# Edge sort: where and when the passed rows are marked

## The chip, the cores and the metric

The kernel runs on one core of a Trainium2 chip. The metric is the device time of one execution in microseconds; lower is better.

## The reference

```python
# x: 6250 nodes x 256; src, dst: 106250 edges
edge_index = stack([src, dst])
def gnn(X, (row, col)):
    denom = max(segment_sum(1, row), 1)
    neigh_mean = segment_sum(X[col], row) / denom
    H = relu(X @ W_root + neigh_mean @ W_neigh + b)
    diffs = abs(H[row] - H[col]) ** 2
    return tanh(segment_sum(diffs, row) / denom)
x = x + gnn(layernorm(x), edge_index)
x = x + mixture_of_experts(layernorm(x))   # router, 6 experts of 3 layers, the best 2 combined
```

Edges arrive sorted by `dst` and are summed by `src`, so the kernel first sorts them itself.

## The kernel before

The nodes lie in 49 blocks of 128. The kernel has four stages, one after the other: the edge sort (to about 297 us), a first pass over 842 tiles of 128 edges that sums neighbours, a second pass over the same tiles that sums squared differences, and the experts. In both passes GpSimd gathers the rows of a tile by an indirect DMA, VectorE makes a one-hot matrix, TensorE multiplies, VectorE adds the product to the block's sums.

The change is in the edge sort. The edges stand as 128 lanes by 832 columns. After ranks are found (VectorE, GpSimd and ScalarE, to about 105 us), the edges are put in order chunk by chunk. There are `C` = 8 chunks with two halves each, `CC` = 16 lists. `dve_edges` (line 858) runs 64 steps `k` of `BT` = 13 columns; four steps (`t` = 0 to 3) make a list. In a step VectorE makes three one-hot operands: `is_col` (line 993), `hot_lane` (line 997) and `hot_col` (line 1001; ScalarE makes 8 of its 13 upper columns, line 812). TensorE multiplies them into a list in PSUM (line 728). At `t` = 2 of the next list VectorE and ScalarE move the finished list to SBUF (`dve_list`, line 1123; `act_low`, line 856). At `k` = 3 VectorE also makes the variances of the nodes (lines 1194 to 1181).

Each list has 512 rows of 16 edges, 4 groups (`GG`) of 128. A row's place in DRAM depends on which blocks begin before it. For each of the first 8 chunks VectorE marks, for 98 half blocks and 512 rows, three times whether the row number has passed a start (`dve_passed`, line 1117, one instruction of 98 x 1536 in step `t` = 0). TensorE multiplies the marks with the jumps of the row numbers (`pe_rows`, line 776, at `t` = 1), and VectorE sums that to places (`dve_rows`, lines 1131 and 1134, at `t` = 3). All chunks use one tile `passed`.

GpSimd (`pool_edges`, line 582) makes 14 of the 49 bucket masks (line 649), the counting rows `count_h` (line 653), and then scatters: for each of 16 lists, it waits for places and list, and issues 4 indirect DMAs of 128 rows each to DRAM, which add (line 663). 64 scatters in all. Lists alternate between two DRAM tables. After the last, SyncE loads the two tables back (`sp_list`), TensorE turns them, VectorE makes indices, and GpSimd's first gather starts (line 1276).

SyncE meanwhile writes the normalised rows for the gathers (line 1141), four blocks at a time, and behind each of the first ten writes it clears a part of the sums' tile `big` (`sp_clear`, lines 561 and 563). The parts lie behind `sorting_end`, where the working tiles of the sort end. VectorE clears the rest after the sort (line 1211).

The order on every engine is that of the program; engines are tied by semaphores alone.

Of the kernel before, what the change touches and what calls it, by code (L numbers as in the profile page):

```python
# [38 lines left out]
def gnn_moe_kernel(nc, x, x_cols, x_cols_last, src, dst, w_root, w_neigh, b_gnn, rw1, rb1, rw2, rb2,  # L39
# [66 lines left out]
    with ExitStack() as ctx:  # L106
# [121 lines left out]
        passed = carve_sort(3 * GG * P // 2).bitcast(F16).rearrange("p (j r) -> p j r", j=3)  # L228
# [12 lines left out]
        sorting_end = at  # L241
        assert codes_at + 2 * NT <= sorting_end
# [22 lines left out]
        def turned_at(k):  # L265

            bank, place = divmod(k + per - 1, per)
            return ps[bank][:, place * P if bank else 0:][:, 0:min(P, NT - list_blocks[k] * P)]
        by_block = acc.rearrange("p (b w) -> p b w", w=W2)
# [154 lines left out]
        s_passed = sem("passed_rows_marked")  # L424
        s_jumped = sem("row_jumps_summed")
# [130 lines left out]
        assert clear_parts < len(z_sets)  # L556

        def sp_clear(e, i):
            if i == 0:
                e.wait_ge(s_pick, NB)  # L560
                e.dma_start(acc[:, NB * W2 - clear_over:NB * W2], local[:, 0:clear_over]).then_inc(s_cleared, 16)
            a, z = i * CLEAR_BY, min((i + 1) * CLEAR_BY, clear_times)
            e.dma_start(acc[:, sorting_end + a * NTR:sorting_end + z * NTR].rearrange("p (n w) -> p n w", w=NTR),
                        local.unsqueeze(1).to_broadcast([P, z - a, NTR])).then_inc(s_cleared, 16)
# [17 lines left out]
        def pool_edges(e):  # L582
# [71 lines left out]
            e.iota(far, [[CODE, MIX]], base=0, channel_multiplier=CODE * ((N - MIX) // P), **ALL_ONE).then_inc(s_region, 1)  # L654
            for c in range(CC):
# [114 lines left out]
        def pe_rows(e, c):  # L770
            e.wait_ge(s_passed, c + 1)
            if c:
                e.wait_ge(s_dest, c)
            for g in range(GG):
                for j in range(3):
                    m = e.matmul(ps[6][:, 4 * g:4 * g + 4], passed[0:NB2, j, g * P:(g + 1) * P],
# [81 lines left out]
        def dve_edges(e):  # L858
# [125 lines left out]
            e.tensor_scalar(at_rank, iota[0:NB, 0:NB], block_t[0:NB, 4:5], None, ALU.is_equal).then_inc(s_jump, 1)  # L984
            e.tensor_copy(code_f, high[:, :, 0]).then_inc(s_code, 1)
            e.wait_ge(s_wide, 1)
            for k in range(TW // BT):
# [15 lines left out]
                if t == 0 and c < C:  # L1003
                    dve_passed(e, c)
# [107 lines left out]
        def dve_passed(e, c):  # L1112
            if c == 0:
# [3 lines left out]
            e.tensor_tensor(passed[0:NB2, :, :].rearrange("p j (r q) -> p j r q", q=2),  # L1117
                            count_h[0:NB2, :].rearrange("p (r q) -> p r q", q=2).unsqueeze(1).to_broadcast(every),
                            starts_two[:, :, c, :].unsqueeze(2).to_broadcast(every), ALU.is_ge).then_inc(s_passed, 1)
# [1296 lines left out]
```

## Time and profile before

| | |
|---|---|
| median of 3 runs | 2837.13 us (2836.13 to 2838.58) |
| profiled execution | 2836.03 us, its span 2834.2 us |
| busy in the span | TensorE 81%, GpSimd 72%, VectorE 70%, ScalarE 31% |
| masks and ranks end, steps begin | 111.7 us |
| first scatter, last scatter begin | 134.14 us, 289.89 us |
| first gather of the first pass | 297.14 us |

The shares are means over stages with different limits; a stage has to be read from its own rows. An instruction's idle time before it names what released it; "issue" is time for which the profile shows no wait. Overlapping starts (an instruction that begins 0.08 us before the one ahead of it ends) are usual on VectorE, so costs on its path are taken from start to start.

### The profile page before, as it was taken

The numbers are of one execution on the slowest core, as the hardware profiler recorded it, in microseconds if no ns is written. First come the engines' busy times: TensorE is split into PE (matmuls) and PEld (weight loads), VectorE is DVE, ScalarE is ACT, GpSimd is POOL, SyncE is SP. The second block draws the span as 40 slices with busy tenths as digits, with TensorE's granted clock in tenths as the row PEclk, the third lists the DMA queues.
The fourth block names the chain that finished last, engine by engine and source line by source line (L and its number), as shares of the span: only waits on it lengthen the run. The fifth ranks groups of instructions, "written<-read, shape, count | busy, mean of one in ns | idle before, by whom it ended". The sixth has DMA issues, their size and how long they took to land.

```text
span 2834.2 us, 33557 instructions
## 1 busy us (share of the span) xinstructions
PE 2298.4 (81%) x8655; PEld 1296.3 (46%) x8655; DVE 1993.5 (70%) x5304; ACT 872.4 (31%) x2404; POOL 2030.8 (72%) x2021
## 2 busy tenths in 40 slices
PE   6676577777777777777789898888998888899996
PEld 4564444454434444444233333333333333389996
DVE  8997555556655555555578888888888888755456
ACT  7897000001100000000233333333333333355553
POOL 2488777777777777777677777777777766667772
PEclk8598789987677776766899999999999999999998
DMA  4254333334433333333543434344434333332266
GB/s 128 92 143 81 95 106 106 105 106 120 127 105 113 112 113 105 113 112 113 173 119 112 126 118 126 112 124 117 126 112 123 117 93 112 104 102 94 90 190 207
DMA packets 173026, 332.36 MB, mean 117 GB/s; under 512 B 45296, under 2 KB 108636, under 8 KB 172578
## 3 DMA queue, kind: packets, MB, share of 16 engines
q0 software_dynamic: 100224, 249.16, 30.6%
q1 hardware_dynamic: 70306, 78.94, 8.5%
q10 hardware_dynamic: 2304, 2.10, 0.2%
q8 instruction: 71, 1.16, 0.2%
q14 instruction: 121, 0.99, 0.1%
HBM read 279.94 MB, written 40.96 MB: 113 GB/s over the span
## 4 chain that ended last, share of the span: by engine, by line
DVE 28%; PE 24%; POOL 17%; issue 13%; DMA 10%; DVEq 6%; ACT 1%; SPq 0%; POOLq 0%; ACTq 0%
DVE big L1369 19%; PE ps L1320 15%; POOL arena L1276 11%; DMA arena<-xn_table,graph 7%; DVEq L1333 6%; PE ps L2294 5%; POOL edge_list L663 4%; DVE graph L1363 4%; PE ps L2276 3%; DMA arena<-h_table,graph 2%; POOL arena L1803 1%; PE ps L1379 1%; POOL y_by_token L1809 1%; PE ps L2244 1%; DVE big L872 1%
## 5 line engine op out<-in xcount | busy, mean ns | idle before, releaser
L1320 PE MATMUL ps<-arena,graph 128*128 128x258 f32 (+3 forms) x3956 | 1672.7, 593 | 405.9 <-DVE graph L1363 383.8
L1320 PEld LDWEIGHTS ps<-arena,graph 128*128 128x128 f32 (+1 forms) x3956 | 749.9, 223 | 1286.5 <-DVE graph L1363 1025.6
L1369 DVE TENSOR_TENSOR big<-ps,big 128x258 f32 (+1 forms) x1978 | 1100.2, 556 | 112.9 <-PE ps L1320 78.1
L1276 POOL DMA_INDIRECT arena<-h_table,graph x842 | 819.2, 973 | 287.9 <-issue 155.9
L1276 POOL DMA_INDIRECT arena<-xn_table,graph x842 | 799.0, 949 | 261.9 <-issue 191.9
L1363 DVE TENSOR_SCALAR graph<-iota,graph 128x128 f32<-128x128 f32 x1684 | 506.1, 301 | 509.9 <-DMA arena<-xn_table,graph 311.1
L1300 ACT ACTIVATE arena<-arena 128x256 f32<-128x256 f32 x842 | 348.5, 416 | 694.6 <-DMA arena<-h_table,graph 636.0
L1290 ACT ACTIVATE late<-late 128x256 f32<-128x256 f32 x49 | 20.3, 415 | 995.9 <-DVE late L1445 995.9
L1809 POOL DMA_INDIRECT y_by_token<-big,node x106 | 121.0, 1141 | 71.9 <-DVE big L1864 55.1
L663 POOL DMA_INDIRECT edge_list<-big x64 | 138.1, 2158 | 42.9 <-issue 42.3
L1803 POOL DMA_INDIRECT arena<-xn_table,node x106 | 111.8, 1055 | 39.4 <-issue 31.4
L812 ACT ACTIVATE big<-arena,big 128x64 f16<-128x64 f16 x512 | 129.7, 360 | 13.7 <-DVE arena L993 13.5
L1864 DVE TENSOR_TENSOR big<-ps,node 128x256 f32<-128x256 f32 x106 | 45.0, 424 | 118.9 <-PE ps L2276 118.3
L2276 PE MATMUL ps<-node,big 128*128 (+1 forms) x448 | 116.1, 382 | 5.9 <-DVE big L1864 3.5
L2294 PE MATMUL ps<-arena 128*128 128x128 f32 x848 | 114.6, 279 | 0.7 <-ACT big L2183 0.4
L2294 PE MATMUL ps<-big,arena 128*128 128x128 f32 x848 | 112.7, 276 | 0.0
L2294 PEld LDWEIGHTS ps<-arena 128*128 128x128 f32 x848 | 105.3, 195 | 1.9 <-issue 1.7
L2294 PEld LDWEIGHTS ps<-big,arena 128*128 128x128 f32 x848 | 104.0, 193 | 0.0
L728 PE MATMUL ps<-big,arena 128*128 128x128 f16 x832 | 67.7, 239 | 40.8 <-ACT big L812 27.6
L728 PEld LDWEIGHTS ps<-big,arena 128*128 128x128 f16 x832 | 57.2, 108 | 62.1 <-issue 49.8
L1840 DVE COPY arena<-node 128x1028 f32 x106 | 74.4, 703 | 15.4 <-ACT big L2191 6.5
L2276 PEld LDWEIGHTS ps<-node,big 128*128 128x128 f32 x448 | 76.5, 191 | 13.4 <-issue 6.4
(330 smaller groups left out, 1579.3 us busy)
## 6 DMA issues: line engine op xcount, KB each, us to landing
arena<-xn_table,graph POOLq DMA_INDIRECT x842, 2.8
arena<-h_table,graph POOLq DMA_INDIRECT x842, 2.8
big<-y_by_token SPq DMA_DIRECT2D x48, 256.0 KB, 4.4
big<-graph SPq DMA_DIRECT2D x10, 848.0 KB
h_table<-late SPq DMA_DIRECT2D x49, 128.0 KB, 2.1
late<-h_table SPq DMA_DIRECT2D x49, 128.0 KB, 3.0
xn_table<-late SPq DMA_DIRECT2D x12, 512.0 KB
big<-in_x SPq DMA_DIRECT2D x48, 128.0 KB, 2.6
```

What stands on the lines that cost most here:

```text
L663: e.indirect_dma_start(out=edge_list[c % 2], out_offset=bass.IndirectOffsetOnAxis(ap=dest[:, c, g:g + 1], axis=0), in_=lists[:, c, g * R8: ...
L812: e.activation(hot_col[:, r, u, 0, :], is_col[:, r, u, :], ACT.Copy, scale=code_f[:, t0 + u:t0 + u + 1]).then_inc(s_hcola, 1)
L1276: e.indirect_dma_start(out=row, out_offset=None, in_=table, in_offset=bass.IndirectOffsetOnAxis(ap=idx[:, t:t + 1], axis=0)).then_inc(s_ro ...
L1300: e.activation(rows2[:, sq, :], rows2[:, slot, :], ACT.Square).then_inc(s_sq, 1)
L1320: e.matmul(out_, hot[part, g % HOTS, :], moving, start=True, stop=True).then_inc(s_sum[i], 1)
L1333: _, places = nc.values_load_multi_w_load_instructions(offs[0:1, a:z], engines=[mybir.EngineType.DVE], min_val=0, max_val=(NB - 1) * W2, s ...
L1363: e.tensor_scalar(hot[:, g % HOTS, :], iota[:, :], local[:, t:t + 1], None, ALU.is_equal).then_inc(s_hot[i], 1)
L1369: e.tensor_tensor(block, ps[a % n_banks][:, 0:width], block, ALU.add)._wait_ge(s_sum[i], a + 1).then_inc(s_add[i], 1)
L1803: e.indirect_dma_start(out=xg[:, k % XR, :], out_offset=None, in_=xn_table, in_offset=bass.IndirectOffsetOnAxis(ap=tok[:, k:k + 1], axis=0 ...
L1809: e.indirect_dma_start(out=y_table, out_offset=bass.IndirectOffsetOnAxis(ap=y_row[:, k:k + 1], axis=0), in_=y_out[:, k % YB, :], in_offset ...
L2276: m = e.matmul(ps[3][:, 0:D], h2[:, n % 2, j * P:(j + 1) * P], last_of[j], start=(j == 0), stop=(j == KH - 1))
L2294: t = e.matmul(bank[:, m * P:(m + 1) * P], weights_of(k, at_, P), moving[:, j * P:(j + 1) * P], start=(j == 0), stop=(j == KD - 1))
```

## The change

- Each of the 8 chunks gets marks of its own, `passed(c)`, in `big` behind `sorting_end`, 768 words per chunk. A copy of the starts in float32, `starts_f`, lies behind them.
- VectorE copies the starts (one instruction of 98 x 24 ahead of the first step) and marks chunks 0, 1 and 2 in steps `k` = 0, 1, 2, with the same instruction as before (`mark_passed`).
- GpSimd marks chunks 3 to 7, after `count_h` and ahead of its first scatter: three `tensor_scalar` of 98 x 512 per chunk, 15 in all.
- `pe_rows` waits for one semaphore or the other, by chunk.
- The parts cleared by SyncE come in another order: parts 4 to 9, then 0 to 3, and before part 0 (issued behind the seventh write) SyncE waits until the row products of all 8 chunks are made.

```diff
--- before.py
+++ after.py
@@ -225,7 +225,6 @@
         dest_f = carve_sort(2 * GG).rearrange("p (h g) -> p h g", h=2)
         dest = carve_sort(CC * GG).bitcast(U32).rearrange("p (c g) -> p c g", c=CC)
         count_h = carve_sort(GG * P // 2).bitcast(F16)
-        passed = carve_sort(3 * GG * P // 2).bitcast(F16).rearrange("p (j r) -> p j r", j=3)
         ends_t = carve_sort(NB2)
         seen = carve_sort((STEP_COLS + UNITS) * NB)[0:STEP_ROWS, :]
         seen_whole = seen[:, 0:STEP_COLS * NB].rearrange("p (r b) -> p r b", b=NB)
@@ -239,6 +238,9 @@
         code_f = carve_sort(TW)
         hot_col = carve_sort(BT * 2 * HI).bitcast(F16).rearrange("p (r t a m) -> p r t a m", r=2, t=BT, a=2)
         sorting_end = at
+        PASSED_EARLY = 3
+        passed_words = 3 * GG * P // 2
+        assert sorting_end + C * passed_words <= NB * W2
         assert codes_at + 2 * NT <= sorting_end
         assert PR == ZR and 2 * KD * D + ZR * D <= 6 * KD * D and Z_AT + NB < TW // BT
         XAT = -(-taken // D)
@@ -266,6 +268,13 @@
 
             bank, place = divmod(k + per - 1, per)
             return ps[bank][:, place * P if bank else 0:][:, 0:min(P, NT - list_blocks[k] * P)]
+        starts_f = big[0:NB2, sorting_end + C * passed_words:sorting_end + C * passed_words + 3 * C].rearrange(
+            "p (j c) -> p j c", j=3)
+
+        def passed(c):
+            at_ = sorting_end + c * passed_words
+            return big[0:NB2, at_:at_ + passed_words].bitcast(F16).rearrange("p (j r) -> p j r", j=3)
+
         by_block = acc.rearrange("p (b w) -> p b w", w=W2)
 
 
@@ -422,6 +431,7 @@
         s_kept = sem("sums_of_units_kept")
         s_jump = sem("row_jumps_and_ends_made")
         s_passed = sem("passed_rows_marked")
+        s_passed_p = sem("passed_rows_marked_by_pool")
         s_jumped = sem("row_jumps_summed")
         s_dest = sem("list_rows_made")
         s_scat = [sem(f"rows_scattered_{i}") for i in range(2)]
@@ -554,11 +564,16 @@
         clear_times, clear_over = divmod(NB * W2 - sorting_end, NTR)
         clear_parts = -(-clear_times // CLEAR_BY)
         assert clear_parts < len(z_sets)
+        PASSED_PARTS = -(-(C * passed_words + 3 * C) // (CLEAR_BY * NTR))
+        assert PASSED_PARTS < clear_parts
 
         def sp_clear(e, i):
             if i == 0:
                 e.wait_ge(s_pick, NB)
                 e.dma_start(acc[:, NB * W2 - clear_over:NB * W2], local[:, 0:clear_over]).then_inc(s_cleared, 16)
+            i = (i + PASSED_PARTS) % clear_parts
+            if i == 0:
+                e.wait_ge(s_jumped, C)
             a, z = i * CLEAR_BY, min((i + 1) * CLEAR_BY, clear_times)
             e.dma_start(acc[:, sorting_end + a * NTR:sorting_end + z * NTR].rearrange("p (n w) -> p n w", w=NTR),
                         local.unsqueeze(1).to_broadcast([P, z - a, NTR])).then_inc(s_cleared, 16)
@@ -652,6 +667,12 @@
             e.wait_ge(s_pick, NB)
             e.iota(count_h, [[1, GG * P]], base=0, channel_multiplier=0, **ALL_ONE).then_inc(s_region, 1)
             e.iota(far, [[CODE, MIX]], base=0, channel_multiplier=CODE * ((N - MIX) // P), **ALL_ONE).then_inc(s_region, 1)
+            e.wait_ge(s_jump, 6)
+            e.wait_ge(s_region, 11)
+            for c in range(PASSED_EARLY, C):
+                for j in range(3):
+                    e.tensor_scalar(passed(c)[:, j, :], count_h[0:NB2, :], starts_f[:, j, c:c + 1], None,
+                                    ALU.is_ge).then_inc(s_passed_p, 1)
             for c in range(CC):
                 e.wait_ge(s_dest, min(c, C - 1) + 1)
                 e.wait_ge(s_list, c + 1)
@@ -768,12 +789,15 @@
             m.then_inc(s_zP, 1)
 
         def pe_rows(e, c):
-            e.wait_ge(s_passed, c + 1)
+            if c < PASSED_EARLY:
+                e.wait_ge(s_passed, c + 1)
+            else:
+                e.wait_ge(s_passed_p, 3 * (c - PASSED_EARLY + 1))
             if c:
                 e.wait_ge(s_dest, c)
             for g in range(GG):
                 for j in range(3):
-                    m = e.matmul(ps[6][:, 4 * g:4 * g + 4], passed[0:NB2, j, g * P:(g + 1) * P],
+                    m = e.matmul(ps[6][:, 4 * g:4 * g + 4], passed(c)[:, j, g * P:(g + 1) * P],
                                  jumps[:, j, c, :, :].rearrange("p h d -> p (h d)"), start=(j == 0), stop=(j == 2))
             m.then_inc(s_jumped, 1)
 
@@ -982,6 +1006,7 @@
 
             e.tensor_scalar(ends_t[0:NB2, :], ident[0:NB2, 0:NB2], end_of, None, ALU.mult).then_inc(s_jump, 1)
             e.tensor_scalar(at_rank, iota[0:NB, 0:NB], block_t[0:NB, 4:5], None, ALU.is_equal).then_inc(s_jump, 1)
+            e.tensor_copy(starts_f, starts_two[:, :, :, 0]).then_inc(s_jump, 1)
             e.tensor_copy(code_f, high[:, :, 0]).then_inc(s_code, 1)
             e.wait_ge(s_wide, 1)
             for k in range(TW // BT):
@@ -1000,8 +1025,8 @@
                 for i, part, u in ((0, high, BY_ACT), (1, low, 0)):
                     e.tensor_tensor(paired(hot_col[:, r, u:BT, i, :]), paired(is_col[:, r, u:BT, :]),
                                     across(part, t0 + u, BT - u, HI), ALU.mult).then_inc(s_hcold, 1)
-                if t == 0 and c < C:
-                    dve_passed(e, c)
+                if k < PASSED_EARLY:
+                    mark_passed(e, k, s_passed)
                 if t == 2 and c:
                     dve_list(e, c - 1)
                 if t == 3 and c < C:
@@ -1109,14 +1134,14 @@
                 e.tensor_tensor(jumps[:, :, :, :, d], a.unsqueeze(3).to_broadcast([NB2, 3, C, 2]), halves,
                                 ALU.mult).then_inc(s_jump, 1)
 
-        def dve_passed(e, c):
+        def mark_passed(e, c, made):
             if c == 0:
                 e.wait_ge(s_region, 11)
                 e.wait_ge(s_jump, 3)
             every = [NB2, 3, GG * P // 2, 2]
-            e.tensor_tensor(passed[0:NB2, :, :].rearrange("p j (r q) -> p j r q", q=2),
+            e.tensor_tensor(passed(c).rearrange("p j (r q) -> p j r q", q=2),
                             count_h[0:NB2, :].rearrange("p (r q) -> p r q", q=2).unsqueeze(1).to_broadcast(every),
-                            starts_two[:, :, c, :].unsqueeze(2).to_broadcast(every), ALU.is_ge).then_inc(s_passed, 1)
+                            starts_two[:, :, c, :].unsqueeze(2).to_broadcast(every), ALU.is_ge).then_inc(made, 1)
 
         def dve_list(e, c):
             e.wait_ge(s_lowp, c + 1)
```

## Rows read from the trace of the kernel before

**Rows 1.** Stretch in us, its length; busy us (count) of PE, PEld, DVE, ACT, POOL; clock, DMA.

```profile
255.00:297.00 42.00, 14.21 (x108) 12.25 (x108) 13.54 (x29) 12.58 (x52) 30.95 (x19) 0.54 0.29 25
```

**Rows 2.** Chain of waits between 110 and 300 us, shares by line.

```profile
by line: POOL edge_list L663 60.7%; issue 25.0%; DMA edge_list<-big 6.2%; DVE big L1001 1.7%; DMA big<-edge_list 1.3%; DVE arena L993 1.1%; DVE arena L979 1.0%; DVE big L1029 0.6%; DVE big L1023 0.6%; DVE big L1117 0.5%; PE ps L742 0.4%; DV
```

**Rows 3.** GpSimd in order: start us, us, what, [idle before]; last, its 64 scatters (min/median/max ns).

```profile
134.14 3.02 POOL L663 DMA_INDIRECT edge_list<-big  x1 [23.74 <-issue]
...
139.65 4.90 POOL L663 DMA_INDIRECT edge_list<-big  x1 [0.30 <-issue]
...
149.11 5.42 POOL L663 DMA_INDIRECT edge_list<-big  x1 [0.30 <-issue]
...
189.02 5.42 POOL L663 DMA_INDIRECT edge_list<-big  x1 [0.30 <-issue]
...
194.75 2.00 POOL L663 DMA_INDIRECT edge_list<-big  x1 [0.31 <-issue]
...
254.80 1.55 POOL L663 DMA_INDIRECT edge_list<-big  x1 [0.30 <-issue]
...
289.89 1.55 POOL L663 DMA_INDIRECT edge_list<-big  x1 [0.30 <-issue]
...
297.14 1.02 POOL L1276 DMA_INDIRECT arena<-xn_table,graph  x1 [5.71 <-DVE graph L1231]
...
L663 POOL DMA_INDIRECT edge_list<-big x64: 1546/1871/5417, 134.1 to 289.9; - x64
```

**Rows 4.** Gathers of the first pass: duration min/median/max ns, first and last start us.

```profile
L1276 POOL DMA_INDIRECT arena<-xn_table,graph x842: 942/946/1179, 297.1 to 1351.3; - x169
```

**Rows 5.** VectorE in order of time, same columns as rows 3.

```profile
113.88 0.95 DVE L1117 TENSOR_TENSOR big<-big,small 98x1536 f16<-98x1536 f16 x1
...
114.75 0.58 DVE L993 TENSOR_TENSOR arena<-graph,arena 128x832 f16<-128x832 f16 x1
...
121.55 1.75 DVE L1194 BATCH_NORM_AGGREGATE mv<-stats 128x2 f32<-128x6 f32 x25
...
125.67 0.58 DVE L993 TENSOR_TENSOR arena<-graph,arena 128x832 f16<-128x832 f16 x1
...
133.06 0.22 DVE L1123 SCALAR_TENSOR_TENSOR big<-ps,big 128x64 f32<-128x64 f32 x1
...
147.80 0.95 DVE L1117 TENSOR_TENSOR big<-big,small 98x1536 f16<-98x1536 f16 x1
...
153.02 0.22 DVE L1123 SCALAR_TENSOR_TENSOR big<-ps,big 128x64 f32<-128x64 f32 x1
...
195.25 0.16 DVE L1131 SCALAR_TENSOR_TENSOR big<-ps,rownum 128x8 f32<-128x8 f32 x1
...
265.39 0.21 DVE L1123 SCALAR_TENSOR_TENSOR big<-ps,big 128x64 f32<-128x64 f32 x1
```

**Rows 6.** Masks on GpSimd, columns as in rows 4.

```profile
L649 POOL TENSOR_SCALAR arena<-node x10: 2286/2287/2325, 59.5 to 91.6; 128x832 f16<-128x832 f16 x10
```

**Rows 7.** ScalarE in order of time: its last instruction of a chunk.

```profile
209.56 0.22 ACT L856 ACTIVATE big<-ps 128x64 f32<-128x64 f32 x1
...
218.71 0.24 ACT L856 ACTIVATE big<-ps 128x64 f32<-128x64 f32 x1
```

**Rows 8.** SyncE in order of time: the seventh write of normalised rows.

```profile
203.26 0.37 SPq L1141 DMA_DIRECT2D xn_table<-late  x1
```

**Rows 9.** VectorE's column compare of all 64 steps, columns as in rows 4.

```profile
L993 DVE TENSOR_TENSOR arena<-graph,arena x64: 577/584/623, 111.7 to 265.5; 128x832 f16<-128x832 f16 x64
```

**Rows 10.** All engines in order of time, first 8 us.

```profile
1.19 1.27 DVE L862 CAST graph<-iota 128x128 f16<-128x128 f32 x1 [0.21 <-POOL iota L583]
...
6.42 0.18 POOL L619 MEMSET node<- 128x98 f32 x1
...
7.13 0.69 DVE L864 TENSOR_SCALAR node<-arena 128x832 int32<-128x832 int32 x1 [4.67 <-DMA arena<-in_dst]
...
7.41 0.54 POOL L629 MEMSET node<- 128x98 f32 x1
```

## The prediction

> **What bounds the kernel now.** I read the trace in four looks: the busy shares by stretch, the chain of waits over the sorting stage, GpSimd's instructions in order of time, and VectorE's and ScalarE's beside them.
>
> From 255 to 297 us GpSimd is busy for 31 of the 42 us and VectorE for only 13.5: the sort's own work is over, the scatters are behind [rows 1]. The chain runs mostly over the scatter line of GpSimd, 60.7% of its length between 110 and 300 us; the 0.3 us hand-overs between scatters appear there as "issue" [rows 2]. The first gather of the next stage follows the last scatter by a fixed tail: 289.89 + 1.55 = 291.44 us to 297.14 us, 5.7 us [rows 3]. That stage is GpSimd's too: 842 gathers from 297.1 to 1351.3 us, 1.25 us each with no room to catch up [rows 4]. So each microsecond by which the last scatter ends earlier or later should reach the end of the kernel whole.
>
> Inside the scatters there are two paces. From 134.14 to 194.75 us GpSimd issues 18, or 3.37 us each. From 194.75 to 254.80 it issues 27, or 2.22 us each, and the last eleven, with VectorE idle, come every 1.85 us. The slow part is made by six long ones: 4.90 us for the one at 139.65 and 5.42 us for the five others, of which 149.11 and 189.02 stand as first and last [rows 3]. Each starts 1.3 to 1.9 us after one of VectorE's eight marks of passed rows (line 1117, the mark at 147.80 for the scatter at 149.11), and ends 1.3 us after the next list instruction of VectorE (153.02 + 0.22 against 154.53) [rows 3, 5]. Behind the eighth and last mark comes one such scatter, that at 189.02, and then none. Between marks and long scatters the count is six for six. The other two marks lie ahead of the first scatter.
>
> **The change part by part.** *Marks that leave the scatters.* Six of eight marks now stand between scatters. In the changed kernel three are made in VectorE's steps 0 to 2, all ahead of the first scatter, and five by GpSimd, also ahead of it. A mark costs VectorE 0.87 us (113.88 to 114.75) [rows 5]; five fewer give 4.35 us. Ahead of the first list stand three instead of two, so that list comes 0.87 us later.
>
> *The copy of starts.* One cast of 98 x 24 on VectorE. The nearest row is an instruction of 128 x 8 with 0.16 us (195.25) [rows 5], about 0.1 us from start to start. The bounds are 0.05 and 0.25.
>
> *Fifteen marks on GpSimd.* The trace has no such instruction of 98 x 512 f16; the nearest is its compare of 128 x 832 f16, 2.287 us [rows 6]. In proportion to the columns that is 1.41 us; a small fixed part makes it more, and I take 1.47. The 832-column row itself, 2.29, is the upper end; a third of it, 0.76, is a lower end. Fifteen make 22.1 us (11.4 to 34.3). They start once the starts are copied, at about 111.5, and would end at 133.6. GpSimd has just this gap: it idles 23.74 us ahead of the scatter at 134.14 [rows 3]. So alone they cost nothing; if they took 2.29 us each, the scatters would begin 11 us late. TensorE's products for a chunk wait for these marks from step 13 on, after 145 us, so they are in time.
>
> *What the freed scatters do.* The list of chunk 0 moves from 133.06 to 134.03, and the first scatter, 1.08 us behind it as now [rows 3, 5], to 135.1. From there GpSimd needs 53 x 2.22 + 11 x 1.85 + 1.2 (its first is longer, 3.02 us) = 139.2 us, and would end at 274.3. But it can't be ahead of the lists. These come every 9.98 us now (133.06 to 153.02 is two), and without the mark VectorE needs 9.11; ScalarE needs 9.16 per chunk (209.56 to 218.71) [rows 5, 7] and becomes the slower by a hair, which takes back some 0.3 us of the 4.35. The list of chunk 14 moves from 265.39 to 265.39 - 4.35 + 0.1 + 0.3 = 261.4. Chunk 14's scatters then start at 262.5 and take 4 x 2.1 = 8.4, chunk 15's 4 x 1.85 = 7.4: end at 278.3. This is the later of the two, so it holds: 291.4 - 278.3 = 13.1 us less. The wait on VectorE's lists is what is late next. The lower and upper ends of this part are 17.1 (GpSimd's own pace) and, if GpSimd's marks run at 2.29 us, 291.4 - 285.4 = 6.0 (first scatter at 146.2, plus 139.2).
>
> *The order of the clears.* The same bytes are cleared by the same eleven DMAs; parts 4 to 9 come first, and the seventh, issued behind the write at 203.26, now waits until all eight row products are made. VectorE uses the eighth at 195.25 [rows 5, 8], so the wait is over 8 us before. Queued behind it on SyncE are the normalised rows' writes, which the first gather needs; were the wait late, they would be late by as much, with 80 us in hand. Zero.
>
> *Rows of their own.* A chunk's marks no longer overwrite those that TensorE reads; no wait was seen for that, so nothing is gained.
>
> *The sum.* The profiled execution took 2836.03 us (span 2834.2 and 1.8 around it). 2836.0 - 13.1 = 2822.9; the median of the runs, 2837.1, is 1.1 above the profiled one, so 2824.0.
>
> **What speaks against it: a shared way into the memory.** The scatters' lengths show that GpSimd waits for VectorE when it reads. The least of the 64 is 1.546 us and the last ones, alone, are as short; the median, beside VectorE's steps, is 1.871, and the long ones last until VectorE runs something else [rows 3]. In the other direction the trace shows little: VectorE's compare of 832 columns is 577 ns at the least and 623 at the most over all 64, with 45 scatters beside it [rows 9]; but a scatter reads only 128 offsets. At the start of the kernel both directions stand once. A GpSimd memset of 98 columns takes 0.54 us beside VectorE's shift of 832 columns, and 0.18 otherwise. A VectorE cast of 128 columns takes 1.27 us beside GpSimd's first memsets, where that shift of 832 takes 0.69 [rows 10]. A mark on GpSimd reads its 512 columns throughout, so it could shut VectorE out for its whole 1.47 us.
>
> The Trainium skill says so outright (SBUF — State Buffer, "Who interferes with whom"): a VectorE instruction with two SBUF inputs contends with a GpSimd instruction that reads SBUF, and whoever holds the shared pair keeps it for the whole instruction. The trace agrees for GpSimd's reads (1.546 against 1.871 us); for VectorE being held for a whole GpSimd compare no row here shows it, and by the rule the time would be that of the first rival below.
>
> **The rivals.**
> 1. *The two engines take turns (slower).* Every instruction of VectorE's steps has two inputs in SBUF. If each GpSimd mark holds one up for its length, VectorE loses 22.1 us before its first list, or 18.0 if marks lie beside the variances (121.55 to 125.67 [rows 5]), which mostly read one input. All lists move with it: the end of the scatters is 278.3 + 18.0 to 22.1 = 296.3 to 300.4, that is 4.9 to 9.0 us later than now. It decides from 13.1 us of hold-up, that is from 0.9 us per mark. For it: the rows above. Against it: VectorE's times beside 45 scatters. With 7.5 us: 2844.6.
> 2. *GpSimd starves.* It gets in once per step of 2.17 us. If VectorE loses nothing, 15 marks last 15 x 2.17 = 32.6 us, the first scatter starts at 144.4 and the last ends at 283.6, 7.8 us less than now: 2829. This is still my side of the line. If it is both starved and holds VectorE up (2.17 + 1.47 = 3.64 us per mark from step 4 on, if 8 are left then: 133.4 + 29.1), the first scatter starts near 162.5 and the last ends near 301.7: 2847.
> 3. *The marks are not what makes the scatters long.* Then three scatters pass per chunk for the first six chunks as now, at 9.11 instead of 9.98 us each: 5.2 less, 1.0 later start, so 4.2: 2833. Against it: the six-for-six count. It is also the case in which the change doesn't do what it says.
>
> **How the numbers follow.** Forecast, with the milder half of rival 2: 0.53, its own range 2820 to 2830. Rival 1: 0.29. The harsh half of rival 2: 0.06. Rival 3: 0.12. A measurement of this kernel can tell 0.2%, 5.7 us, from no change. Faster by more than that: the forecast's 0.53 and 0.02 of rival 3, 0.55. Within: the rest of rival 3 and a quarter of rival 1, 0.17. Slower: 0.28. The range 2819 to 2847 takes in both signs and leaves out the harsh end and gains above 18.
>
> **What would show it.** Right: no scatter above 2.5 us but the first; 15 GpSimd compares of about 1.5 us from 111.5 on, ended by 134; VectorE's 832-column compares still near 584 ns between 112 and 134; list of chunk 0 at 134; last scatter ended near 278; the gathers 13 us earlier with the same pace. Wrong by rival 1: instructions of VectorE between 112 and 145 that last up to 2 us, first list after 150. By rival 2: compares of GpSimd longer than 2 us. By rival 3: scatters of 5 us although no mark stands near them.

## The result, and the profile after

The changed kernel takes 2843.29 us (median of 11 runs, 2840.54 to 2846.14), the kernel before 2837.16 us in its runs beside it (11 runs, 2835.97 to 2844.02). The ratio is 1.0020 with a 95% interval of 1.0012 to 1.0028: slower, by 6.1 us where 13.1 us less were forecast. The profiled execution took 2841.83 us, its span 2840.1 us.

The busy shares by stretch answer to [rows 1]; the columns are the stretch and its length, then the busy time of TensorE, its weight loads, VectorE, ScalarE and GpSimd with the instructions in brackets, the granted clock, and the DMA share and rate.

```profile
110.00:134.00 24.00, 9.25 (x84) 7.85 (x85) 23.59 (x71) 12.20 (x49) 22.98 (x9) 0.50 0.66 268
255.00:297.00 42.00, 13.09 (x118) 11.37 (x118) 14.34 (x29) 14.29 (x60) 33.23 (x20) 0.60 0.25 15
```

GpSimd was to finish its fifteen marks in the first of these stretches. It has nine instructions there, seven of them marks, and is busy from the first mark on. At the end of the sort the picture is as before: VectorE is idle for two thirds of the stretch, and scatters are still being issued.

GpSimd in order of time answers to [rows 3] (start and duration in us, engine, line, operation, operands, count; in brackets its idle time before it and what ended that):

```profile
109.47 0.56 POOL L668 IOTA big<- 128x512 f16 x1
111.19 43.18 POOL L674 TENSOR_SCALAR big<-big 98x512 f16<-98x512 f16 x15 [1.02 <-DVE big L1009]
154.55 2.02 POOL L684 DMA_INDIRECT edge_list<-big  x1 [0.18 <-issue]
...
292.47 1.55 POOL L684 DMA_INDIRECT edge_list<-big  x1 [0.30 <-issue]
300.03 1.02 POOL L1301 DMA_INDIRECT arena<-xn_table,graph  x1 [6.01 <-DVE graph L1256]
```

The marks last 43.18 us instead of 22.1. The first scatter starts at 154.55, where 135.1 was forecast and 134.14 stood before; the last ends at 294.02 instead of 291.44, and the first gather starts at 300.03 instead of 297.14 [rows 3].

By line, with the least, the median and the longest duration in ns and the first and last start, the fifteen marks and the 64 scatters are:

```profile
L674 POOL TENSOR_SCALAR big<-big x15: 1559/2107/13136, 111.2 to 152.3; 98x512 f16<-98x512 f16 x15
L684 POOL DMA_INDIRECT edge_list<-big x64: 1546/1958/2227, 154.6 to 292.5; - x64
```

The long scatters of 5.42 us are gone, as forecast. What took their place is a first mark of 13.14 us and fourteen others of 2.1 us mostly; 1.56 us is the least. Cut down to its start, the first mark reads

```profile
111.19 13.14 POOL L674 TENSOR_SCALAR big<-big 98x512 f16<-98x512 f16 x1 [1.02 <-DVE big L1009]
```

and it ends at 124.33. VectorE beside it answers to [rows 5]:

```profile
110.92 0.16 DVE L1009 CAST big<-small 98x24 f32<-98x24 f16 x1
113.68 0.94 DVE L1142 TENSOR_TENSOR big<-big,small 98x1536 f16<-98x1536 f16 x1
...
119.76 0.94 DVE L1142 TENSOR_TENSOR big<-big,small 98x1536 f16<-98x1536 f16 x1
...
122.81 0.15 DVE L1156 SCALAR_TENSOR_TENSOR big<-ps,rownum 128x8 f32<-128x8 f32 x1
122.99 0.16 DVE L1159 TENSOR_TENSOR big<-big,ps 128x8 uint32<-128x8 f32 x1
...
125.38 0.53 DVE L1194 TENSOR_SCALAR nsc<-nsc 128x49 int32<-128x49 int32 x1
...
129.78 1.24 DVE L1026 TENSOR_TENSOR big<-arena 128x320 f16<-128x320 f16 x2
...
136.14 0.21 DVE L1148 SCALAR_TENSOR_TENSOR big<-ps,big 128x64 f32<-128x64 f32 x1
...
159.27 0.81 DVE L1026 TENSOR_TENSOR big<-arena 128x320 f16<-128x320 f16 x2
```

Two things are to be seen. First, from 111.19 to 122.96 VectorE's instructions follow each other with overlapping starts and the mark does not move. Between the row sum at 122.81 and the next at 122.99 there are 0.03 us in which VectorE runs nothing, and the mark ends 1.37 us after that. Counted from the start of the row sum at 122.81 it is 1.52 us. The long scatters of the kernel before end 1.50 to 1.51 us after the start of a list instruction (153.02 for the one at 149.11), and there the next instruction starts at 153.15, before the list instruction's 0.22 us are over [rows 3, 5]. So a gap of VectorE is not needed: what the list instruction and the row sum have in common is that they read PSUM and only one tile in SBUF. Second, once the marks do get in, VectorE is held up, but lightly: the pair of `hot_col` products takes 1.23 us beside a mark and 0.81 without one, and an instruction of the variances 0.53 instead of the usual 0.19. It is 0.34 to 0.43 us each time, and not the whole mark. The first mark of GpSimd starts 2.49 us ahead of VectorE's first (113.68), so it is already waiting when that one comes.

The chain of waits between 110 and 300 us, summed by line, answers to [rows 2]:

```profile
by line: POOL edge_list L684 53.5%; issue 19.1%; POOL big L674 12.1%; DMA edge_list<-big 4.0%; DVE big L1026 2.4%; DVE arena L1018 1.6%; DMA big<-edge_list 1.6%; DVE big L1142 1.4%; DVE arena L1003 1.0%; DVE mv L1219 0.9%; DVE nsc L1198 0.5
```

The scatter line fell from 60.7%, and the marks on GpSimd came in with 12.1%: between them they leave VectorE only single per cents.

### The profile page after: what moved, and what is told of

Its sections match the earlier page's. It is cut to its first block, busy times and chain, and to the rows that moved or that the text cites. A ratio compares the mean times of both kernels' runs of the same rounds, so it can differ in the third digit from the quotient of the medians.

```text
span 2840.1 us, 33570 instructions
## 1 busy us (share of the span) xinstructions
PE 2303.5 (81%) x8655; PEld 1299.7 (46%) x8655; DVE 1995.7 (70%) x5300; ACT 871.9 (31%) x2404; POOL 2056.0 (72%) x2036
## 4 chain that ended last, share of the span: by engine, by line
PE 29%; DVE 26%; POOL 16%; issue 12%; DMA 10%; DVEq 5%; ACT 1%; SPq 1%; ACTq 0%; POOLq 0%
PE ps L1345 18%; DVE big L1394 16%; POOL arena L1301 11%; DMA arena<-xn_table,graph 7%; PE ps L2319 6%; DVEq L1358 5%; POOL edge_list L684 4%; DVE graph L1388 3%; PE ps L2301 3%; DMA arena<-h_table,graph 2%; DMA big<-y_by_token 1%; POOL big L674 1%; PE ps L1404 1%; PE ps L2269 1%; PE ps L2344 1%
## 5 line engine op out<-in xcount | busy, mean ns | idle before, releaser
L1345 PE MATMUL ps<-arena,graph 128*128 128x258 f32 (+3 forms) x3956 | 1678.8, 591 | 401.0 <-DVE graph L1388 379.1
L836 ACT ACTIVATE big<-arena,big 128x64 f16<-128x64 f16 x512 | 129.7, 362 | 15.9 <-DVE arena L1018 15.7
L684 POOL DMA_INDIRECT edge_list<-big x64 | 120.3, 1879 | 19.4 <-issue 19.1
L749 PE MATMUL ps<-big,arena 128*128 128x128 f16 x832 | 66.2, 236 | 44.7 <-ACT big L836 15.7
```

The lines of the kernel that those rows point to most:

```text
L684: e.indirect_dma_start(out=edge_list[c % 2], out_offset=bass.IndirectOffsetOnAxis(ap=dest[:, c, g:g + 1], axis=0), in_=lists[:, c, g * R8: ...
L749: m = e.matmul(ps[4 + c % 2][:, 0:2 * HI], hot_lane[:, r, u, :], hot_col[:, r, u, :, :].rearrange("p a m -> p (a m)"), start=(t == 0 and u ...
L836: e.activation(hot_col[:, r, u, 0, :], is_col[:, r, u, :], ACT.Copy, scale=code_f[:, t0 + u:t0 + u + 1]).then_inc(s_hcola, 1)
L1345: e.matmul(out_, hot[part, g % HOTS, :], moving, start=True, stop=True).then_inc(s_sum[i], 1)
```

## The experiments

The theory after the result: GpSimd's reads of SBUF find a place only at certain instructions of VectorE. Three questions follow. Is it GpSimd's marks that cost the time (e1)? What in VectorE's mark shuts GpSimd out: its place (e2), its form with two inputs (e3), the lack of an instruction behind it that would break the run (e4)? Or is it that VectorE, whose mark waits for nothing, gets ahead of its own instruction stream, so that a next instruction always stands ready (x1 and what follows)?

The x and y kernels ran on two other chips, on which the kernel before takes 3160 us; so each ratio is against the kernel before on the same chip. There is no trace of the kernel before from those chips, and times inside the sort are compared across chips. That the sort keeps its times there is seen at x1, which has before's marks in before's places and starts its first scatter at 133.74 (134.14 before).

### e1: all eight chunks marked by VectorE ahead of the scatters

```diff
-        PASSED_EARLY = 3
+        PASSED_EARLY = 8
```

> The changed kernel with all eight chunks marked by VectorE, one in each of steps 0 to 7, and none by GpSimd. Theory A (GpSimd's marks wait for VectorE; a VectorE mark closes the way to GpSimd until VectorE's next instruction that is not a two-input one of the step): no starved marks, the first list 0.87 x 5 us after that of before (137.4), first scatter at 138.5, one long scatter at most (marks of steps 6 and 7), last scatter ended at 278 to 282 against 291.4 before and 294.0 changed: about 2837 - 11 = 2826 us. Theory B (the marks on VectorE are not what makes scatters long; any step does it while the first eight chunks run): the six long scatters stay, time 2837 to 2842 us.

Measured: 2829.5 us, ratio 0.9971 (0.9961 to 0.9982). GpSimd in order of time, and VectorE around the first scatter:

```profile
138.94 3.76 POOL L684 DMA_INDIRECT edge_list<-big  x1 [28.30 <-DVE big L1148]
...
280.46 1.55 POOL L684 DMA_INDIRECT edge_list<-big  x1 [0.30 <-issue]
287.95 1.02 POOL L1301 DMA_INDIRECT arena<-xn_table,graph  x1 [5.94 <-DVE graph L1256]
```

```profile
136.86 0.96 DVE L1142 TENSOR_TENSOR big<-big,small 98x1536 f16<-98x1536 f16 x1
137.73 0.23 DVE L1148 SCALAR_TENSOR_TENSOR big<-ps,big 128x64 f32<-128x64 f32 x1
...
140.04 0.96 DVE L1142 TENSOR_TENSOR big<-big,small 98x1536 f16<-98x1536 f16 x1
140.90 0.17 DVE L1156 SCALAR_TENSOR_TENSOR big<-ps,rownum 128x8 f32<-128x8 f32 x1
```

The half of the change that takes marks from between the scatters is worth 7.1 us of the kernel (2829.5 against 2836.6) and 9.2 at the first gather. So GpSimd's fifteen marks cost that gain and 6.1 us more. And two marks here stand beside the start of the scatters without making a 5 us one (the first scatter lasts 3.76 us): the list instruction or the row sums come directly behind them. The time of 2829.5 us lies above the 2826 expected, and the last scatter's end, 282.01, at the edge of 278 to 282.

### e2: the three VectorE marks ahead of the first step

```diff
+            for c in range(PASSED_EARLY):
+                mark_passed(e, c, s_passed)
...
-                if k < PASSED_EARLY:
-                    mark_passed(e, k, s_passed)
```

> The changed kernel with VectorE's three marks moved ahead of its first step, so that no mark stands between the steps; GpSimd's fifteen marks as they are. Theory A: GpSimd's first mark, 13.1 us in the changed kernel, falls to under 4 us, the fifteen together to about 33 us (43.2 now), first scatter near 147, time 5 to 8 us below the changed kernel: 2836 us. Theory B (two-input steps alone keep GpSimd out until the row sums of step 3): the first mark still lasts over 10 us, time within 2 us of the changed kernel's 2843.

Measured: 2843.04 us, ratio 1.0024 (1.0015 to 1.0033). Nothing moved:

```profile
L674 POOL TENSOR_SCALAR big<-big x15: 1557/2105/13129, 111.1 to 152.2; 98x512 f16<-98x512 f16 x15
```

The first mark of GpSimd lasts 13.13 us again, though no mark of VectorE now stands between its steps. This is what theory B said: VectorE's ordinary steps keep a GpSimd instruction that is once waiting out until the row sums of step 3. VectorE's three marks now stand at 110.91 to 113.59, beside the start of GpSimd's. No run starts GpSimd's marks with no VectorE mark near, so what the marks add to the steps is not separated here.

### e3: the marks as one-input instructions

Before's schedule, with marks in rows of their own; each is three `tensor_scalar` on VectorE instead of one `tensor_tensor` with two inputs.

```diff
-        PASSED_EARLY = 3
+        PASSED_EARLY = 8
-                if k < PASSED_EARLY:
-                    mark_passed(e, k, s_passed)
+                if t == 0 and c < C:
+                    mark_passed(e, c, s_passed)
-            e.tensor_tensor(passed(c)..., count_h..., starts_two..., ALU.is_ge).then_inc(made, 1)
+            for j in range(3):
+                e.tensor_scalar(passed(c)[:, j, :], count_h[0:NB2, :], starts_f[:, j, c:c + 1], None,
+                                ALU.is_ge).then_inc(made, 1)
```

> Marks at the places of before (step t = 0 of each of the first eight chunks), all by VectorE, but as three compares of 98 x 512 with one input each instead of one of 98 x 1536 with two; rows of their own; none by GpSimd. Theory A (it is the two-input form of the mark that closes the way): no scatter above 2.5 us but the first, last scatter ended near 279, 2824 to 2828 us. Theory B (whatever stands at that place lets VectorE run on without a gap, or the place itself does it): the six scatters of 5 us stay, 2836 us give or take what the shorter marks save (2 us).

Measured: 2839.85 us, ratio 1.0015 (1.0006 to 1.0024). GpSimd's long scatters stay, six of them, the last at 189.16; VectorE's three marks stand 1.3 us ahead of the one at 148.59:

```profile
148.59 5.58 POOL L684 DMA_INDIRECT edge_list<-big  x1 [0.31 <-issue]
...
189.16 5.58 POOL L684 DMA_INDIRECT edge_list<-big  x1 [0.30 <-issue]
```

```profile
147.28 1.12 DVE L1143 TENSOR_SCALAR big<-big 98x512 f16<-98x512 f16 x3
148.32 0.58 DVE L1018 TENSOR_TENSOR arena<-graph,arena 128x832 f16<-128x832 f16 x1
```

The `tensor_scalar` form of the mark shuts GpSimd out as the two-input one does. It is one form with one input: list instructions and row sums, which read PSUM, let GpSimd in. All six long scatters here end 1.50 to 1.51 us after the start of a list instruction, as before.

### e4: one small copy behind each mark

```diff
+            e.tensor_copy(small[0:NB2, 3 * C:3 * C + 1], ident[0:NB2, 0:1]).then_inc(s_v, 1)
```

> The kernel before, with one copy of 98 x 1 behind each of the eight marks and nothing else changed. Theory A: the one-input copy opens the way, the six long scatters fall to about 2 us; first scatter at 134.3, VectorE's lists 0.7 us later at the end, last scatter ended near 283: about 2829 us. Theory B: the long scatters stay at 5 us and the time at 2837 to 2839 us.

Measured: 2839.32 us, ratio 1.0007 (0.9998 to 1.0016). VectorE has the copy, and GpSimd the same long scatter:

```profile
147.75 0.95 DVE L1117 TENSOR_TENSOR big<-big,small 98x1536 f16<-98x1536 f16 x1
148.62 0.15 DVE L1120 COPY small<-ident 98x1 f32<-98x1 f32 x1
148.68 0.59 DVE L993 TENSOR_TENSOR arena<-graph,arena 128x832 f16<-128x832 f16 x1
```

```profile
149.06 5.47 POOL L663 DMA_INDIRECT edge_list<-big  x1 [0.30 <-issue]
```

This small copy is no opening. That it overlaps both neighbours (148.68 is ahead of 148.62 + 0.15) does not explain it, for the list instruction at 153.03 overlaps its neighbours too, and the scatter ends 1.51 us after that one's start.

### x1 and y4: VectorE waits for each of its marks

The kernel before, with one wait behind each mark, for the mark itself. y4 is the same kernel, timed again on another chip.

```diff
                             ALU.is_ge).then_inc(s_passed, 1)
+            e.wait_ge(s_passed, c + 1)
```

> The kernel before, with VectorE waiting for the end of each mark before it issues the next instruction; nothing else. Theory Q (GpSimd gets in only where VectorE's next instruction was not already waiting behind the running one; a mark without waits of its own gives VectorE's queue a lead that lasts until the next list or row sum): the wait takes the lead away, the six scatters of 5.4 us fall below 3 us, last scatter ended near 282, 2828 us. Theory P (only where a scatter's request falls in the step's pattern decides; the mark shifts the pattern by 0.87 us): the eight waits change VectorE's times by 0.1 us each, the long scatters stay, 2837 us.

> The kernel before with eight waits and nothing else, timed in more rounds: on another chip its last scatter ended 10.2 us earlier than that of the kernel before here, so the ratio should be 0.9955 to 0.997, 2826 to 2829 us where before takes 2837. Theory against it: the passes that follow (TensorE's clock, their start) give half of it back, ratio 0.998 to 0.999.

Measured: x1 3151.07 us, ratio 0.9958 (0.9939 to 0.9977); y4 3146.36 us, ratio 0.9949 (0.9929 to 0.9968). The scatters of y4 by line, three of them, and VectorE around the mark (before's mark in this step is followed by its next instruction after 0.87 us, here after 0.98):

```profile
L663 POOL DMA_INDIRECT edge_list<-big x64: 1546/1871/3014, 133.9 to 279.9; - x64
```

```profile
139.45 2.12 POOL L663 DMA_INDIRECT edge_list<-big  x1 [0.30 <-issue]
...
154.01 2.86 POOL L663 DMA_INDIRECT edge_list<-big  x1 [1.12 <-issue]
...
286.93 1.02 POOL L1277 DMA_INDIRECT arena<-xn_table,graph  x1 [5.52 <-DVE graph L1232]
```

```profile
137.62 0.95 DVE L1117 TENSOR_TENSOR big<-big,small 98x1536 f16<-98x1536 f16 x1
138.60 0.59 DVE L993 TENSOR_TENSOR arena<-graph,arena 128x832 f16<-128x832 f16 x1
...
153.06 0.22 DVE L1124 SCALAR_TENSOR_TENSOR big<-ps,big 128x64 f32<-128x64 f32 x1
```

Eight waits take away all six long scatters. The scatter that lasted 4.90 us at 139.65 [rows 3] lasts 2.12 here, at 139.45. It starts 0.9 us after the gap behind the mark (138.57 to 138.60), so it does not profit from the gap itself: it gets in among ordinary steps, as scatters do that are far from a mark. From the third list to the seventh the lists now set the start of their scatters: 1.12 us of idle time at 154.01, 0.95 us behind the list at 153.06. The first gather comes at 286.93 instead of 297.14, which is 0.32% of 3160 us. y4's ratio is below the 0.9955 to 0.997 that was expected, but its interval reaches there; the theory against it, 0.998 to 0.999, is out.

That the wait is the cure is shown. That it works by taking away a lasting lead of VectorE's queue, as theory Q says, is not. Ahead of each column compare VectorE's sequencer waits at line 992. Here is that wait for the two steps behind the mark at 147.80 in the kernel before, then behind that at 147.72 in y4 (ns least/median/most, first and last start), with the compares that follow it:

```profile
L992 DVEq EVENT_SEMAPHORE  x2: 21/21/21, 149.3 to 151.5; - x2
...
150.84 0.58 DVE L993 TENSOR_TENSOR arena<-graph,arena 128x832 f16<-128x832 f16 x1
...
153.15 0.58 DVE L993 TENSOR_TENSOR arena<-graph,arena 128x832 f16<-128x832 f16 x1
```

```profile
L992 DVEq EVENT_SEMAPHORE  x2: 21/21/21, 149.4 to 151.5; - x2
...
150.89 0.59 DVE L993 TENSOR_TENSOR arena<-graph,arena 128x832 f16<-128x832 f16 x1
...
153.20 0.58 DVE L993 TENSOR_TENSOR arena<-graph,arena 128x832 f16<-128x832 f16 x1
```

In both kernels the sequencer is ahead of these two compares by the same 1.54 and 1.67 us, since each step waits for its own column compare (`s_iscol`) anyway. Yet in y4 a scatter gets in there and in the kernel before none does. What differs is GpSimd: before, its scatter has been waiting since 149.11; in y4 one got in behind the mark, and the next starts at 151.03:

```profile
151.03 1.87 POOL L663 DMA_INDIRECT edge_list<-big  x1 [0.31 <-issue]
...
159.13 1.69 POOL L663 DMA_INDIRECT edge_list<-big  x1 [0.30 <-issue]
```

Where a scatter starts in the step, theory P's point, does not decide alone either. Behind marks that VectorE does not wait for, scatters that start 0.27 (e3), 0.38 (e4) and 0.44 us (before) into the next compare are all drawn out to about 5.5 us; the one at 159.13, 0.32 us into the compare behind a mark waited for, takes 1.69.

### x2: a wait in every step

```diff
             for i, part, u in ...
+                if i:
+                    e.wait_ge(s_hcold, 2 * k + 1)
```

> The kernel before, with VectorE waiting in each of its 64 steps for the end of its first column product before it issues the second, so that its queue runs empty once a step. Theory Q: GpSimd gets in at that place, no scatter above 2.6 us but the first; the steps grow by 0.05 to 0.1 us each (3 to 6 us in all); last scatter ended at 283 to 287, 2829 to 2833 us. Theory P: long scatters stay, or come in other places, and the time grows by the wait: 2837 to 2842 us.

Measured: 3151.89 us, ratio 0.9968 (0.9950 to 0.9986). No scatter is longer than 3.10 us, the median grows to 1.997, and the wait costs VectorE 0.13 us in each of 64 steps (the pair of products takes 0.94 instead of 0.81). The last list comes at 276.1 instead of 269.5, and the last scatter at 285.94 where y4 has 279.87: six of its ten microseconds are paid back. The expectation was missed in part: it had no scatter above 2.6 us but the first, and six take 3.09 or 3.10. They still end within the steps, not with a list.

### x3: the changed kernel with that wait in its first 16 steps

```diff
+                    if i and k < 16:
+                        e.wait_ge(s_hcold, 2 * k + 1)
```

> The changed kernel (three marks by VectorE, fifteen by GpSimd) with the same wait in VectorE's first 16 steps. Theory Q: GpSimd's first mark, 13.1 us in the changed kernel, falls to 2 to 3 us; fifteen marks in 32 to 36 us instead of 43.2, first scatter at 144 to 149, 5 to 9 us below the changed kernel: 2835 to 2838 us. Theory P: the first mark stays over 10 us, 2843 us or more.

Measured: 3159.04 us, ratio 0.9982 (0.9965 to 0.9999).

```profile
L674 POOL TENSOR_SCALAR big<-big x15: 1559/2503/3557, 110.8 to 144.8; 98x512 f16<-98x512 f16 x15
```

The mark of 13 us is gone (3.56 at most), and the scatters start at 147.60 instead of 154.55. But the others pay: the first four take 3.50 to 3.56 us each (the first was expected at 2 to 3), the median is 2.50 where 2.11 stood, and all fifteen take 36.6 us, a little above the 32 to 36 expected.

### x4: six chunks by VectorE, two by GpSimd

```diff
-        PASSED_EARLY = 3
+        PASSED_EARLY = 6
```

> The changed kernel with six chunks marked by VectorE, in steps 0 to 5, and two by GpSimd (six compares). If GpSimd's pace is as in the changed kernel (first mark 13 to 14 us, then 1.6 us beside the variances and 2.2 to 2.6 us per step), its six marks end at 134 to 136, ahead of the first list at 136.5, and the first scatter starts at 137.6: last scatter ended near 281, 2828 us, 1 to 2 us below the kernel with all eight on VectorE (2829.5). If more marks on VectorE keep GpSimd out longer than 13 us (theory Q allows it: one lead after another up to the row sums of step 3, at 123.7), the first scatter starts up to 2 us later: 2830 us. Theory that any use of GpSimd here costs more than a mark on VectorE: above 2833 us.

Measured: 3150.09 us, ratio 0.9972 (0.9946 to 0.9998).

```profile
L674 POOL TENSOR_SCALAR big<-big x6: 1555/2042/14004, 111.1 to 132.2; 98x512 f16<-98x512 f16 x6
```

```profile
132.19 7.02 POOL L674 TENSOR_SCALAR big<-big 98x512 f16<-98x512 f16 x1
```

The long first mark is there with six instructions as with fifteen, and the sixth is a second long one. It starts at 132.19, beside VectorE's mark at 131.70, stays out past the one at 134.74, and ends at 139.21, 1.43 us after the start of the first list instruction (137.78). So GpSimd's marks were done at 139.2 and not at 134 to 136 as expected, and the first scatter starts at 139.39, behind them and not behind the list, beside e1's 138.94; the last ends at 282.74 (281 expected), and the first gather comes at 288.80 beside e1's 287.95. In the whole kernel x4 isn't told apart from e1. GpSimd's marks are free only as long as they fit ahead of the first list.

### y1, y2, y3: the changed kernel with waits behind VectorE's marks, and 3, 5 or 7 chunks on VectorE

```diff
+            e.wait_ge(made, c + 1)
```

(behind the instruction of `mark_passed`; y2 and y3 also with PASSED_EARLY = 5 and 7)

> The changed kernel (three marks by VectorE, fifteen by GpSimd), with VectorE waiting for the end of each of its three marks. By theory Q GpSimd's first mark gets in behind VectorE's first (114.6 us): 4 to 5 us instead of 13.1; fifteen marks in 35 to 38 us, first scatter at 147 to 149.5, last scatter ended at 287 to 290 against 294.0: a ratio to before of 0.999 to 1.000. If only a wait in every step helps (and not one at the mark), the first mark stays at 12 us or more and the ratio at 1.002.

> As y1, with five chunks marked by VectorE (steps 0 to 4) and three by GpSimd (nine compares). GpSimd's nine marks at 2.2 to 2.6 us each after a first of 4 to 5 us end by 134 to 137, no later than the first list; first scatter at 137 to 138.5; last scatter ended at 279.5 to 281.5; ratio 0.9955 to 0.997. If VectorE's hold-ups of 0.4 us per GpSimd mark add up on the lists, the last scatter ends at 283: no better than six and two (282.8).

> As y1, with seven chunks marked by VectorE (steps 0 to 6) and one by GpSimd (three compares, done by 120). If VectorE's total work sets the end (the scatters now wait for the lists), two more marks than in y2 make it 1.7 to 2 us later: last scatter ended at 281.5 to 283. If GpSimd's hold-ups cost more than the marks they save, it is the earlier of the two: under 280.

Measured: y1 3153.19 us, ratio 0.9968 (0.9951 to 0.9986); y2 3148.01 us, 0.9969 (0.9952 to 0.9986); y3 3148.79 us, 0.9963 (0.9944 to 0.9983). GpSimd's marks by line in y1, its first mark there, and VectorE beside that:

```profile
L674 POOL TENSOR_SCALAR big<-big x15: 1557/2090/4877, 111.9 to 143.1; 98x512 f16<-98x512 f16 x15
```

```profile
111.91 4.88 POOL L674 TENSOR_SCALAR big<-big 98x512 f16<-98x512 f16 x1 [1.18 <-DVE big L1009]
```

```profile
114.40 0.95 DVE L1142 TENSOR_TENSOR big<-big,small 98x1536 f16<-98x1536 f16 x1
115.38 0.96 DVE L1018 TENSOR_TENSOR arena<-graph,arena 128x832 f16<-128x832 f16 x1
...
117.21 1.23 DVE L1026 TENSOR_TENSOR big<-arena 128x320 f16<-128x320 f16 x2
```

y1 adds three waits to the changed kernel and turns +0.20% into -0.32%. The first mark of GpSimd ends at 116.79, 1.44 us after VectorE's first gap at 115.35, and VectorE pays for it in the next instruction (0.96 us instead of 0.57). All fifteen take 33.13 instead of 43.18 us, and the first scatter starts at 145.23. The 10.05 us come from the first mark (8.3 us shorter) and from the others beside the following steps. All of this is better than expected: 35 to 38 us for the marks, first scatter at 147 to 149.5, ratio 0.999 to 1.000. The first gather, at 292.19, is 4.95 us ahead of before's, 0.16% of 3160 us, so the sort explains half of the 0.32%.

y2 missed its expectation: its scatters were to start at 137 to 138.5 and start at 140.5, and to end at 279.5 to 281.5 and end at 284.4. Its nine marks are done at 131.2, so they are not late; its lists are. The first comes at 139.5 instead of e1's 137.7, though two marks fewer stand ahead of it, and the scatters follow it. That is VectorE's hold-ups of 0.42 us, two per step (the products at 120.60 and the instruction behind the mark), and the waits. y3 ended at 282.65, as expected.

In sum, the last scatter ends at 281.2 us in x1 and 281.4 in y4, the same kernel, 282.0 in e1, 282.65 in y3, 282.7 in x4, 284.4 in y2, 286.4 in y1, 287.5 in x2, 289.5 in x3, 291.4 in the kernel before and 294.0 in the changed kernel. By this the wait alone is the best version run, and it needs no other part of the change. y4's ratio and e1's overlap at the interval's ends (0.9929 to 0.9968 and 0.9961 to 0.9982), so in the whole kernel the two aren't told apart.

## Why the prediction was wrong

*What bounds the kernel* was right: GpSimd's scatters up to the first gather, with a fixed tail (5.7 us before, 6.0 after). The later passes give some of a shift back, though: the first gather was 2.9 us late, the last gather of the second pass 1.5 us (2460.5 against 2459.0).

*The marks removed from the scatters* did what was forecast. No long scatter is left, and from the start of the first to the end of the last it takes 294.02 - 154.55 = 139.5 us, where the sum had 139.2. Rival 3 fell with that. That they were long because of the marks was right, but how was not understood: three compares in the place of the mark (e3) and a copy behind it (e4) leave them long, and a wait of VectorE on the mark is the cure (x1). Why the wait cures is open.

*The copy of starts* takes 0.16 us, 0.08 from start to start: as taken. *The order of the clears* cost nothing: the seventh is issued at 205.47, 0.41 us behind its write at 205.06, as before (203.67 behind 203.26).

*The step that failed* is "Fifteen make 22.1 us (11.4 to 34.3) ... and would end at 133.6." They took 43.18 us and ended at 154.37, outside even the bound taken from the 2.29 us row. The mistake was to price them by a compare that GpSimd ran in the stage before the steps; rival 2 had them wait, but let each one in once per step. The least, 1.56 us, is indeed near the 1.47 assumed; the median is 2.11. The missing term was the first, 13.14 us, and the rows that held it stood in the prediction: if a scatter of 1.55 us could be drawn out to 5.42 behind one mark, until the next list, then an instruction that starts where VectorE's marks stand one step after another may be drawn out to the next list or row sum too. The change starts GpSimd's marks just there, 11.6 us ahead of the first row sum (111.19 to 122.81).

*The rivals.* The sum had neither engine held up; its chance of 0.53 took in the mild half of rival 2, 32.6 us of marks. That rival's direction was right, GpSimd starves, but the size was 43.2. Rival 1's time, 2844.6, is near the measured one, and its mechanism is wrong: VectorE's first list came at 136.14, 2.1 us later than the forecast 134.03, and not 18 to 22. The hold-up is about 0.4 us per mark. The lists did not gate: that of chunk 14 came at 266.86 (261.4 forecast), 27 us ahead of the end of the scatters. By the Trainium skill (SBUF — State Buffer, "Who interferes with whom") the one that holds the shared pair keeps it for the whole instruction; the trace agrees that VectorE's work keeps GpSimd's reads out, and does not show it in the other direction (VectorE is held up for 0.42 us by a mark of 1.56). It also shows GpSimd waiting for up to 13.1 us over some twenty instructions of VectorE, none longer than about 1 us.

*The arithmetic of the miss.* The fifteen marks ended 20.8 us later than forecast (154.37 against 133.6). The first scatter, which would have followed the list at 135.1, started 19.4 us late, so its end was 274.3 + 19.4 + 0.3 = 294.0: what was measured. The forecast's 278.3 was set by the lists; without that other bound the miss would have been 19.7 us, with it it is 15.7.

*What stays open.* The sort accounts for 2.9 of the 6.1 us. e1, e2 and e3, which share the layout and the clears' order of the changed kernel, are also 2.1, 3.9 and 2.4 us slower than their first gathers say (against 297.14 before), e4, which does not share them, 1.7. That is little more than one execution's scatter; no run was made for it, and the cause isn't settled. In the profiled executions the difference arises behind the second pass: from its last gather to the end the kernel before takes 375.3 us (2458.98 to 2834.2), the changed one 379.6 (2460.48 to 2840.1), e1 383.8, and e2, e3 and e4 377.4 to 379.1; each is one execution. Why a GpSimd instruction, once kept out, stays out over steps in which others get in is open too: the lead of VectorE's queue is the same where they do and where they don't, the place in the step alone doesn't decide, and what the list instruction and the row sum have that e4's copy lacks (an operand in PSUM, a wait for another engine) was not varied. Nor was it tried to start GpSimd's marks at another time.

## What to carry to other kernels

Before work is moved to GpSimd beside a busy VectorE, look for GpSimd's longest instruction of any kind there and for the VectorE instruction that let it end; price the moved work by that and not by its time alone. Where a GpSimd instruction is drawn out, try one wait of VectorE on its own last instruction: here 0.11 us each, eight times, brought 0.4 to 0.5%. A change of two halves is to be timed as two: here one was worth 7 us, and the other cost 13.

## What the runs showed of the hardware

- GpSimd's compares and scatters can be kept out by back-to-back VectorE instructions: a compare of 1.56 us lasted 13.1 us (14.0 in x4), a scatter of 1.55 us 5.4. The eighteen long scatters of before, e3 and e4 end 1.50 to 1.52 us after the start of a list instruction, which overlaps its neighbours, and the first mark of the changed kernel 1.52 us after that of a row sum. Both read PSUM.
- One semaphore wait of VectorE on each of its eight marks costs 0.11 us each, and no scatter then lasts longer than 3.0 us, where six lasted 4.9 to 5.4.
- VectorE loses 0.34 to 0.43 us when a GpSimd compare of 1.56 us gets in, not the compare's length.
- GpSimd's compare of 98 x 512 f16 takes 1.56 us at the least and 2.1 in the median beside VectorE's steps.
